# The same instructions in another order: a new static order of five engines and another choice of PSUM pairs in a hybrid attention and feed-forward block

## The reference, cut to what matters

```python
x = x + attn_a(layernorm(x))   # 32 heads of 16, 8 key heads, 8 batches of 256 rows, rotary, causal
x = x + ffn(layernorm(x))      # base matmul + bias, top-2 of 8 gates, low-rank experts of rank 16
x = x + attn_b(layernorm(x))   # the same attention with other weights
x = x + ffn(layernorm(x))
```

## Time and profile before

| | before |
|---|---|
| median of 3 runs | 701.85 us (700.58 to 702.53) |
| the profiled execution | 700.57 us, its span 698.8 us |
| PE busy | 644.5 us (92%) |
| DVE busy | 567.0 us (81%) |
| POOL busy | 505.7 us (72%) |
| ACT busy | 481.7 us (69%) |
| granted TensorE clock, mean | 0.972 |

### The profile page before, as it was taken

The page is one execution under the profiler, slowest core; times in us unless marked ns, Lnnn a source line. Parts: engine busy times, 40 slices in busy tenths (PEclk is TensorE's granted clock), DMA queues, the critical chain, the costliest instruction groups (busy, mean ns, idle before and its releaser), DMA issues.

```text
span 698.8 us, 20922 instructions
## 1 busy us (share of the span) xinstructions
PE 644.5 (92%) x7488; PEld 495.3 (71%) x7488; DVE 567.0 (81%) x2724; ACT 481.7 (69%) x945; POOL 505.7 (72%) x497
## 2 busy tenths in 40 slices
PE   3959899999999999999999999998899999978997
PEld 3947677686877777687867777876688777755575
DVE  5788879798988789798897969788887977888463
ACT  5756677759577867777678676767487785675741
POOL 3385878678696969988688996938579785873532
PEclk9969899999999999999999999999999999996999
DMA  8474444352635456452556445253543616253111
GB/s 295 121 179 99 125 95 127 101 161 69 171 97 149 125 130 178 128 146 52 166 135 166 122 107 163 66 143 87 134 132 97 173 41 162 83 127 82 40 39 61
DMA packets 51223, 85.17 MB, mean 122 GB/s; under 512 B 8816, under 2 KB 25840, under 8 KB 51120
## 3 DMA queue, kind: packets, MB, share of 16 engines
q1 hardware_dynamic: 51120, 83.84, 44.2%
HBM read 24.04 MB, written 10.42 MB: 49 GB/s over the span
## 4 chain that ended last, share of the span: by engine, by line
PE 48%; POOL 13%; DMA 9%; DVE 9%; SPq 8%; issue 6%; ACT 6%; DVEq 0%; POOLq 0%; ACTq 0%
PE T L420 25%; PE T L512 9%; PE T L484 5%; PE T L498 4%; DVE T L1125 4%; PE T L421 3%; DMA Qs<-Qf 2%; POOL PT L1298 2%; POOL Qs L199 2%; POOL Qf L194 2%; POOL R L210 2%; ACT PT L908 2%; PE T L425 2%; POOL Qf L205 2%; DMA sums<-Lc 2%
## 5 line engine op out<-in xcount | busy, mean ns | idle before, releaser
L1125 DVE CUSTOM_DVE_ANT_0 T<-T,mask 128x256 f32<-128x256 f32 (+1 forms) x1024 | 328.3, 391 | 32.2 <-PE T L484 31.8
L908 ACT ACTIVATE PT<-T 128x1024 f32<-128x1024 f32 x192 | 191.2, 1020 | 32.8 <-PE T L498 31.9
L1298 POOL TENSOR_SCALAR_AFFINE_SELECT PT<-PT 128x1024 f32<-128x1024 f32 x128 | 139.3, 1108 | 26.5 <-ACT PT L908 26.4
L1125 DVE DVE_READ_ACCUMULATOR2_ANT nm<- 128x1 f32 x1024 | 142.6, 139 | 0.0
L420 PE MATMUL T<-XH,WQh 64*128 64x256 f32 x384 | 114.7, 299 | 2.7 <-DVE WQl L150 2.4
L421 PE MATMUL T<-XH,WQh 64*128 64x256 f32 x384 | 114.7, 299 | 0.0
L420 PE MATMUL T<-XL,WQh 64*128 64x256 f32 x384 | 109.3, 285 | 0.0
L421 PE MATMUL T<-XL,WQh 64*128 64x256 f32 x384 | 109.3, 285 | 0.0
L420 PE MATMUL T<-XH,WQl 64*128 64x256 f32 x384 | 109.3, 285 | 0.0
L421 PE MATMUL T<-XH,WQl 64*128 64x256 f32 x384 | 109.3, 285 | 0.0
L484 PE MATMUL T<-QK 64*128 64x256 f32 (+1 forms) x1024 | 95.1, 292 | 12.6 <-DMA QK<-R 7.8
(11 more groups left out here) (140 smaller groups left out, 2395.3 us busy)
## 6 DMA issues: line engine op xcount, KB each, us to landing
QK<-Rh SPq DMA_DIRECT2D x64, 256.0 KB, 3.8
QK<-R SPq DMA_DIRECT2D x64, 160.0 KB, 3.1
Qs<-Qf SPq DMA_DIRECT2D x32, 256.0 KB, 2.4
De<-sums SPq DMA_DIRECT2D x62, 128.0 KB, 2.7
QK<-R SPq DMA_DIRECT2D x64, 64.0 KB, 3.2
mid<-X SPq DMA_DIRECT2D x8, 512.0 KB, 3.8
X<-mid SPq DMA_DIRECT2D x8, 512.0 KB, 4.5
Nu<-EF SPq DMA_DIRECT2D x31, 128.0 KB, 2.5
```

The lines of the kernel that those rows point to most:

```text
L908: e.activation(PT[:, 2 * (k % RING):2 * (k % RING) + 2, :], T[j][:, :, :], ACT.Exp, scale=0.25).then_inc(S["ex"], 1)
L1125: ins = e.tensor_tensor_reduce(t, t, mask[:, 256 - n:256], 1.0, LOWEST, ALU.add, ALU.max, nm[:, p % 2, 0, 8 * a + 2 * g + q:8 * a + 2 * g ...
L1298: e.affine_select(out=blk, in_=blk, compare_op=ALU.is_ge, fill=0.0, base=0, pattern=[[0, 8], [1, 128]], channel_multiplier=-1).then_inc(S[ ...
```

## The change

Each of the five lists is replaced by another order of the same calls. The calls and their counts are the same on every engine; what differs is their place, the PSUM pair `j`, and so the semaphore that a PE call waits for before it writes its pair. No helper is changed. Two lines of the diff as a sample, of PE's list near the start:

```diff
-            vT(1, 2, ("qe2", 2)); A(0, 1, 3, ("al", 5)); front("a", 5, 0, ("qe1", 2)); A(0, 2, 2, ("ve", 2))
-            A(1, 0, 1, ("m", 1)); A(1, 1, 3, ("m", 2)); A(1, 2, 2, ("m", 3)); M2(0, 1, ("m", 4)); M2(1, 3, ("m", 5))
+            M2(0, 2, ("m", 3)); A(1, 2, 0, ("m", 4)); front("a", 5, 2, ("ml", 1)); B(0, 0, 3, ("m", 5))
+            M2(1, 0, ("m", 6)); A(2, 0, 3, ("ex", 1)); B(0, 1, 1, ("al", 5)); B(0, 2, 2, ("al", 6))
```

More of the change, by code:

```diff
@@ L358, in _ @@
[L358 to L367, removed]
@@ L403, in _ @@
[L403 to L406 removed]
+            first(0); first(1); const("iden"); rows(1); load(0); load(1); load(2); load(3); rows(2); load(4); rows(3)
@@ new lines, in _ @@
+            power("a", 8, 2); split_low_p(10); addbias(0); addbias(1); split_low_p(11); causal(7, 2); ra(3, 2)
+            causal(8, 0); causal(8, 2); rs_(3, 0); rc(3, 1); rs_(3, 1); ra(3, 1); mu(2); rc(3, 0); gt(0); fH(0)
+            ra(3, 0); ol(2); causal(9, 0); mu(3); ol(3); rl(3, 1); rl(3, 0); causal(9, 2); causal(10, 0)
+            power("f", 2, 2); causal(10, 2); addbias(2); addbias(3); causal(11, 0); causal(11, 2); rs_(4, 0)
+            rs_(4, 1); rc(4, 0); rc(4, 1); ra(4, 0); ra(4, 1); mu(4); power("a", 10, 2); rs_(4, 2); rc(4, 2); ra(4, 2)
@@ new lines, in _ @@
+            addbias(7); causal(19, 0); causal(19, 2); rs_(6, 2); power("a", 14, 2); causal(20, 0); rc(6, 2); mu(8)
+            ra(6, 2); rc(6, 1); rs_(6, 0); rc(6, 0); ol(8); rs_(6, 1); ra(6, 0); ra(6, 1); gt(3); fH(3); mu(9)
+            causal(20, 2); ol(9); rl(6, 1); rl(6, 0); causal(21, 0); causal(21, 2); causal(22, 0); power("f", 8, 2)
+            causal(22, 2); causal(23, 0); addbias(8); addbias(9); rs_(7, 2); rc(7, 2); causal(23, 2)
+            power("a", 16, 2); split_low_p(17); split_low_p(18); mu(10); ra(7, 2); rc(7, 1); rs_(7, 1); rs_(7, 0)
@@ new lines, in _ @@
+            rl(8, 0); power("f", 12, 2); addbias(12); addbias(13); causal(30, 0); causal(30, 2); causal(31, 0)
+            causal(31, 2); power("a", 20, 2); rs_(9, 0); mu(14); rc(9, 1); rs_(9, 1); rc(9, 0); ra(9, 0); gt(6)
+            rs_(9, 2); causal(32, 0); rc(9, 2); fH(6); ol(14); ra(9, 1); rl(9, 0); mu(15); rl(9, 1); ol(15); ra(9, 2)
+            causal(32, 2); causal(33, 0); causal(33, 2); split_low_p(21); power("f", 14, 2); split_low_p(22)
+            causal(34, 0); split_low_p(23); causal(34, 2); causal(35, 0); addbias(14); addbias(15); rs_(10, 2)
@@ new lines, in _ @@
+            rc(10, 2); split_low_p(24); causal(35, 2); mu(16); power("a", 22, 2); rs_(10, 0); rc(10, 0); rc(10, 1)
+            ol(16); rs_(10, 1); ra(10, 2); gt(7); fH(7); causal(36, 0); ra(10, 1); ra(10, 0); causal(36, 2); mu(17)
+            causal(37, 0); ol(17); rl(10, 1); rl(10, 0); causal(37, 2); causal(38, 0); causal(38, 2)
+            power("f", 16, 2); causal(39, 0); causal(39, 2); rs_(11, 2); rc(11, 2); addbias(16); causal(40, 0)
+            addbias(17); mu(18); ra(11, 2); rs_(11, 0); rc(11, 0); rc(11, 1); power("a", 24, 2); ra(11, 0); rs_(11, 1)
```

1038 lines of the change are left out of this document (514 added, 524 removed).

## The result

The changed kernel is slower: 708.96 us median (707.54 to 711.99, 8 runs) against 702.59 us (699.72 to 705.86, 8 runs) of the kernel before on the same chips, ratio 1.0113, 95% interval 1.0083 to 1.0144. The forecast was 697.5 us. The profiled execution took 708.2 us, its span 706.5 us.

A forecast was written before the change was run, and what follows sets the result against it. PE, busy 644.5 of 698.8 us, was taken as the bound, so only its waits and half clock could gain. Terms -2.0 - 1.0 - 2.4 + 1.0 = -4.4 us from 701.85 gave 697.5 us, range 691 to 705.

The forecast's parts named there:

- The start: Up to the first `B`: `M2(0)` and `ml(0)` start earlier, fewer weight transfers and splits ahead; -2.0 us, bounds 0 and -4.4.
- 60 to 90 us: ACT's `oh(0)` moves behind four more calls, so its wait for `mu(0)` no longer holds up other work; -1.0 us.
- Slot 12: 450 to 500 us: two `causal` and an `addbias` ahead of POOL's swap wait, q's swap sent earlier; -2.4 us.
- The rest of the middle: Other slots, 100 to 600 us: idle stays 1.4 us per stretch; possible new pile-up priced at +1.0 us, bounds 0 and +4.7.
- The sign that I had named for being wrong: 100 to 600 us: PE's idle time grows, which would mean new pile-ups; 15 to 18 us was expected.
- The end: From `PV(28)` on: places and the list behind `PV(31)` as before, POOL without a gap; 0 us, lower bound -3.
- The slower rival: Slot 15's q swap goes out 1.9 to 9.9 us late, or another pile-up elsewhere; 704 to 707.4 us, chance 0.15.
- The clock: Gaps around 75 and 625 us close and two half-clock spells go; 690.7 us at most, 692.5 with part; chance 0.12.

The follow-up runs named there:

- The head alone: New order from the start to just ahead of `PV(16)`, the old order behind it; ratio 0.9977 to the kernel before.
- the best version: Old order with the new one from the start to `PV(16)` and between `PV(20)` and `PV(22)`; 694.77 us, ratio 0.9909 to the kernel before.
- the run with slot 14 alone: Old order with the new one only between `PV(24)` and `PV(27)`; ratio 1.0051 to the kernel before.
- the run with the `addbias` moved: New order, with POOL's `addbias(26)`, `(28)`, `(29)` placed as in the old order, `gt(15)` and `fH(15)` ahead of the last two `addbias`; ratio 1.0046 to the kernel before.
- the run with slots 13 and 14: Old order with the new one only between `PV(21)` and `PV(27)` (some 475 to 590 us); ratio 1.0110 to the kernel before.

## Why the prediction was wrong, step by step

**The start, -2.0 us, and 60 to 90 us, -1.0: not refuted, not shown, and wrong in what was to be seen.** The head alone measured -0.23% (-1.6 us), with an interval from -3.7 to +0.5 that includes both terms and zero. The first turn came at 39.44, a microsecond earlier than announced, and the first `B` at 44.07, at the early end of what was announced; PE waited for 1.39 us right ahead of the latter. But PE's idle time from 20 to 100 us stayed at 12.5 us instead of falling to 10. The gain lies in the clock: the half-clock spell from 39 us is 10.2 us long instead of 17.1, and the mean of 40 to 60 is 0.75 instead of 0.60. For 60 to 90 us nothing is seen: 60 to 80 idles for 3.65 us, 3.3 before. At `PV(2)`, which has the same calls ahead of it, the new order is 2.7 us early.

**Slot 12, -2.4 us: right** (-2.0, interval -3.9 to -0.1), though POOL's wait did not fall below 3 us as announced but rose to 6.17. The number was right and the way to it was not: the wait stayed, and the gain came in spite of it, likely from the work that was put ahead of it.

**The rest of the middle, +1.0 us: the step that failed.** "The number of calls between a producer and its waiter is on the whole as before", so "the common 1.4 us per stretch" would stay, with one chance in ten for a new pile-up. Measured: +5.3 us in slots 9 to 11, +2.8 in slot 13, +3.6 in slot 14, 11.7 in all, over twice my upper bound of 4.7. The sign that I had named for being wrong came true: the idle time of the middle grew, from 18.7 to 23.8 us. A count of calls is an average, while a wait arises where one distance is too short, and the rows show two such places: the swap of 2 us directly ahead of `mr(40)` on SP, and the three calls that no longer stand ahead of `fW(10)`. Neither is proved to be what its slot lost; the second was taken away, and the slot took as long. What is shown is where the losses lie and how large they are. And one pile-up in ten stretches was a count over one order that had been measured, not a rate for another.

**The end, 0: the second step that failed.** I compared PE's list behind `PV(31)`, which is indeed the same, and POOL's only up to `PV(28)`. POOL's four `addbias` cost 0.7% as undone, by rows 3.2 us on DVE. Without them the new end seems to gain (0.9909 to 0.9860 when it is added to the best version, with intervals that overlap).

**Under both lies a premise,** "a reordering can't shorten the work itself: the calls are the same". The calls are the same, but their time is not: DVE needed 9 us more for the same 2724 instructions, and the sum had no term for it.

**The slower rival** named slot 15's swap. SP's rows after, in order of time:

```profile
598.51 1.14 SPq L351 DMA_DIRECT2D QK<-mT  x2
600.94 0.55 SPq L248 DMA_DIRECT2D Qs<-Qf  x1
```

The swap stands behind the maxima as described, and `PV(28)` follows `PV(27)` 1.5 us sooner than before (with one `B` call less ahead of it). In the run with slot 14 alone, which has the new place of the swap and the old order behind it, the swap went out at 601.01 and `PV(28)` followed `PV(27)` by 24.1 us, as before. So the swap costs nothing that can be seen; one trace, that of the run with the `addbias` moved, has 26.0 us there, with a wait of 1.54 us for ACT. What came true is the clause beside it, losses elsewhere in the middle, in three places instead of one. I had given it a part of a chance of 0.15, and its price, 704 to 707.4 us, was too low for the 708.96 measured.

**The clock** did not act as a rival of its own: the mean granted clock is 0.973 in the trace after and 0.972 in that before, so over the whole it neither gave nor took. It was spread otherwise. The start's spell is 6.9 us shorter and the one near 640 is gone, while the one at 630 is 3.4 us longer and two are new, so that five stand ahead of the last microseconds where four did: one (6.8 us from 568.9) comes at the end of the 2.40 us wait that starts at 567.2, the other (3.4 us from 678.1) follows the 2.16 us wait that ends at 676.9. The rule cited in the forecast (the Trainium skill, "TensorE: Matmul & The Clock Gate", section "HAM oscillation": a wait is paid more than once) agrees with both of these, but not with every long wait: the 3.20 us ahead of `fW(10)` in the run with slots 13 and 14 were followed by no half clock.

## What to carry to other kernels

Compare two orders engine by engine and to the end, and look for the shortest distance between a producer and its waiter, not for the mean one; on the queue that starts transfers, look for what was put directly ahead of an urgent one. A small instruction of DVE that works in SBUF is cheap only where POOL has a gap: put it where nothing urgent stands behind it, and keep runs of POOL instructions away from a chain of such DVE instructions. Where two static orders reach the same set of calls, splice them: it prices each part of a change in one run each, and the good parts make a kernel that neither order was.
